# A graph layer's scatter regions: fifteen old pairs in one region of 11 tiles a bucket, read in three parts

## The chip, the cores and the metric

One core of a Trainium2 chip runs the whole kernel. The metric is the time of one execution in device microseconds (us), and the changed kernel is to be compared with the kernel before on it.

## What is computed

One message-passing layer over 3125 nodes of 64 features and 53125 edges (each node has 17 incoming or own edges, sorted by `dst`), all in f32:

```
h = relu(layernorm(x))
msg = concat(h[dst], edge_attr)                 # 53125 x 128
m = relu(msg @ W1a.T + b1a) @ W1b.T + b1b
agg = segment_sum(m, src) / max(count(src), 1)  # by source node
z = relu(concat(h, agg) @ W2a.T + b2a) @ W2b.T + b2b
out = x + concat(z, h) @ Wr.T + br
```

The gather by `dst` is easy, since edges are sorted by it. The sum by `src` is a sum over rows in any order.

## The kernel before

**Groups and pairs.** Edges are worked in 54 groups of 1024, two to a pair, 27 pairs. `ORDER` has a letter for each pair: O for old, C for paired rows. Pairs 0 to 3 are O, then C and O alternate eight times, then seven are O. So groups 8, 9, 12, 13, ..., 36, 37 are C groups, the others O groups.

**The path of a group.** SP loads `dst` (into `dstb`) and the edges (into `eo`). TensorE projects the node window of a pair (`project_windows`), ScalarE copies it to `pw` and makes the window's one-hots in the other half of `eo`; `hidden(g)` is 8 matmuls on TensorE, and `relu(g)` on ScalarE writes their rows to `pay` (old) or `hid` (paired). TensorE and VectorE rank the rows by bucket, of which there are 25 with 125 source nodes each (node modulo 25), and VectorE makes each row's place, `pos_i`. GpSimd then scatters the group's 1024 rows to `slots_dram` in 8 indirect DMAs. In a C group, four `perm` rounds on TensorE bring two rows that go to the same bucket side by side, ScalarE copies them (`copy_unit`), VectorE makes `pos_c` behind the fourth, and GpSimd sends them to `pairs_dram` in 4 indirect DMAs.

**Regions.** `slots_dram` has a region for each of six phases, `PAIRS = [5, 5, 5, 2, 1, 1]` old pairs long; in a region each bucket has `C[ph]` tiles of 128 rows: 4, 4, 4, 2, 1, 1. The paired rows have one region of 3 tiles of double rows a bucket. Since the number of rows that a bucket gets varies, the last `ROOM[ph]` rows of each bucket are cleared first (`clear`, four pieces; `clear_chunks` for the paired), and `check_ranks` sees that each bucket is filled at least to `LEAST[ph]` and not past its end. If a check fails, a slow path computes the layer again; it does not run here.

**Sums.** When a phase's scatters have landed, its region is read back in rounds: `load_round` on SP brings the tiles of 2 or 3 buckets (12 tiles at most, `TPR`) to one of `RR = 4` buffers in `rows`, VectorE makes a one-hot of 128 x 125 for each tile (`hots`), TensorE multiplies one matmul for each tile (`sum_round`), and VectorE adds the round's result to `sums` (`take`). One-hots and results have two buffers, so that round r needs round r - 2 to be done (`hots`) and taken (`sum_round`). Other rounds are `h` and `z` (parts of the output that need no sums), `ccount` and `crank` (ranks of the paired rows), `perm` and `check`.

**What sets the order.** Every engine's program is written out in one order. A planner deals the rounds to groups: `after[g]` are those that come behind `hidden(g)` on TensorE. It has a room in matmuls, fed by 23 a group, by 10 in the first and by -8 behind a C group, and a phase's sums are ready from `END_GROUP[ph] + AFTER_PHASE[ph]`. What doesn't fit is `left_over` and comes behind the last group, and the last phase's rounds are the tail, with the output behind each. On SP, the loads of a group, the clears and the row loads of `after[g - 1]` stand in one queue.

A f32 matmul stands in the trace as two passes (1100 rows at L1252 for 550 sum matmuls). The planner gives the groups around the C groups these sum matmuls before: 24 after 16, 24 after 20, 24 after 24, 12 after 28, 16 after 31, 24 after 36; then 12 after 39, 24 after 40 and 41, 16 after 42, 24 after each of 43 to 48, 6 after 49, 24 after 50 to 52, 28 after 53; 75 are left over in 18 rounds, and 25 are the tail.

## Time and profile before

| | |
|---|---|
| three timed runs, median | 738.26 us (728.47 to 745.05) |
| the profiled execution, its time | 737.99 us |
| its span | 736.3 us |
| mean granted TensorE clock | 0.796 of full |
| PE / PE weight load / DVE / ACT / POOL busy | 66% / 58% / 44% / 38% / 49% |

The span is the part that the hardware profiler records. PE is TensorE, DVE is VectorE, ACT is ScalarE, POOL is GpSimd, SP is the queue that starts most transfers. A row of the timeline gives start, time, engine, line, what is written and read, how many, and in brackets how long the engine stood idle before it and what ended that; "remote" is an end that the trace can't assign, "issue" one without a wait that it shows. Ends of matmuls are modelled, so a row can stand earlier than the result is ready. `oh` is the one-hot tile `oh2`, and `pay<-bank` at L1058 is `copy_unit`.

### The profile page before, as it was taken

The page shows a single profiled execution, that of the slowest core. Times are in us where ns is not written, and L with a number is a line of the kernel's source. Part 1 is how long each engine was busy: PE and PEld are TensorE (multiplying, and loading weights), DVE is VectorE, ACT ScalarE, POOL GpSimd, SP SyncE. Part 2 cuts the span into 40 slices and gives each one's busy share as a digit, 9 for nine tenths or more (in the row PEclk, how much of TensorE's full clock was granted, in tenths as well). Part 3 has the DMA queues.
Part 4 walks back from the last instruction along what each step waited for, and adds up shares of the span by engine and source line. Part 5 has one row for each costly group of instructions (what it writes and reads, how often), then busy time and mean ns, then how long its engine had stood idle before and what let it go on. Part 6 is the DMA issues. An engine that isn't in the chain of part 4 may idle for free.

```text
span 736.3 us, 9578 instructions
## 1 busy us (share of the span) xinstructions
PE 489.4 (66%) x3133; PEld 428.2 (58%) x3133; DVE 325.6 (44%) x1306; ACT 281.1 (38%) x524; POOL 364.3 (49%) x406
## 2 busy tenths in 40 slices
PE   5455369738658478385665865738768876784886
PEld 4344359718456376374554755727758774674775
DVE  7576024214415245043251341614545652573885
ACT  3127326526337245263550761703242343210034
POOL 4766662632725725537355272574656657455000
PEclk9576566859869789598786986968878998797998
DMA  8876655405416227155451651954977866554641
GB/s 196 304 206 180 168 187 161 122 32 186 135 44 223 89 67 260 67 189 169 141 152 51 210 168 59 310 188 142 259 256 236 268 195 229 169 198 137 177 130 47
DMA packets 62323, 123.48 MB, mean 168 GB/s; under 512 B 9369, under 2 KB 33374, under 8 KB 62270
## 3 DMA queue, kind: packets, MB, share of 16 engines
q1 hardware_dynamic: 49598, 91.25, 42.5%
q0 software_dynamic: 12672, 31.58, 12.6%
q8 instruction: 27, 0.44, 0.3%
q14 instruction: 26, 0.21, 0.1%
HBM read 71.53 MB, written 51.25 MB: 167 GB/s over the span
## 4 chain that ended last, share of the span: by engine, by line
PE 52%; issue 23%; DVE 11%; another core or an unknown queue 7%; ACT 5%; DMA 1%; SPq 0%; ACTq 0%; DVEq 0%
PE bank L1252 20%; PE bank L1232 11%; PE bank L1261 9%; DVE oh L771 3%; PE bank L1204 3%; PE bank L1182 3%; ACT pay L1058 1%; PE bank L1285 1%; PE bank L1282 1%; DVE pos L648 1%; DVE slot_t L646 1%; ACT eo L1046 1%; ACT pw L1019 1%; DMA rows<-slots_dram 1%
## 5 line engine op out<-in xcount | busy, mean ns | idle before, releaser
L565 POOL DMA_INDIRECT slots_dram<-pay,pos_i x300 | 293.4, 978 | 148.6 <-issue 89.9
L1252 PE MATMUL bank<-rows,oh 128*125 128x130 f32 x1100 | 179.8, 314 | 110.6 <-issue 92.0
L1252 PEld LDWEIGHTS bank<-rows,oh 128*125 128x125 f32 x1100 | 160.0, 220 | 128.6 <-issue 125.8
L1232 PE MATMUL bank<-pw,eo 128*128 128x128 f32 x856 | 130.2, 310 | 24.8 <-issue 24.1
L548 POOL DMA_INDIRECT pairs_dram<-pay,pos_c x64 | 65.3, 1020 | 161.2 <-DVE pos_c L748 146.5
L1232 PEld LDWEIGHTS bank<-pw,eo 128*128 128x128 f32 x856 | 122.2, 224 | 35.3 <-issue 35.2
L797 DVE TENSOR_TENSOR sums<-sums,bank 125x390 f32<-125x390 f32 (+2 forms) x58 | 29.2, 503 | 204.5 <-remote 148.0
L771 DVE TENSOR_SCALAR oh<-marks,rows 128x125 f32<-128x125 f32 x550 | 114.1, 291 | 3.0 <-DMA rows<-pairs_dram 1.9
L1046 ACT ACTIVATE eo<-dstb,minus_lane 64x256 f32<-64x256 int32 x190 | 85.1, 494 | 54.8 <-issue 27.0
L1261 PE MATMUL bank<-hid,xch 116*128 116x131 f32 (+1 forms) x512 | 69.1, 291 | 21.5 <-ACT pay L1058 13.0
L1035 ACT ACTIVATE pay<-bank 128x1024 f32<-128x1024 f32 (+1 forms) x37 | 37.3, 1007 | 113.2 <-remote 102.4
L1261 PEld LDWEIGHTS bank<-hid,xch 116*128 116x128 f32 (+1 forms) x512 | 65.0, 203 | 25.3 <-ACT pay L1058 15.6
L1051 ACT ACTIVATE eo<-eo,one 64x512 f32<-64x512 f32 x95 | 68.3, 719 | 3.1
L1035 ACT ACTIVATE hid<-bank 128x1024 f32<-128x1024 f32 x16 | 16.4, 1024 | 107.2 <-PE bank L1232 54.3
L1019 ACT COPY pw<-bank 64x512 f32<-64x512 f32 x54 | 31.1, 576 | 66.5 <-remote 63.7
L1182 PE MATMUL bank<-we_in,hT 65*128 65x128 f32 x216 | 37.2, 306 | 18.5 <-issue 18.3
L1182 PEld LDWEIGHTS bank<-we_in,hT 65*128 65x128 f32 x216 | 32.1, 215 | 21.6 <-issue 21.6
L721 DVE TENSOR_SCALAR xch<-slot_no,slot_x 116x256 f32<-116x256 f32 x128 | 37.7, 361 | 0.0
L1058 ACT COPY pay<-bank 128x262 f32<-128x262 f32 x64 | 22.9, 379 | 38.7 <-PE bank L1261 37.3
L748 DVE TENSOR_TENSOR pos_c<-pay,spare 128x4 int32<-128x4 f32 x16 | 2.6, 164 | 75.6 <-ACT pay L1058 75.6
L1282 PE MATMUL bank<-wl,hT 65*125 65x64 f32 x50 | 12.9, 403 | 22.9 <-DVE xr L800 16.2
L1112 ACT ACTIVATE sbar<-tot,cnt 125x128 f32<-125x128 f32 x25 | 8.3, 392 | 47.1 <-DVE cnt L913 47.0
(196 smaller groups left out, 354.7 us busy)
## 6 DMA issues: line engine op xcount, KB each, us to landing
rows<-slots_dram SPq DMA_DIRECT2D x24, 864.0 KB
dstb<-in_dst SPq DMA_DIRECT2D x54, 256.0 KB
eo<-in_edges_T SPq DMA_DIRECT2D x54, 256.0 KB
rows<-pairs_dram SPq DMA_DIRECT2D x12, 864.0 KB
slots_dram<-zeros SPq DMA_DIRECT2D x9, 756.0 KB
slots_dram<-pay,pos_i POOLq DMA_INDIRECT x300
rows<-slots_dram SPq DMA_DIRECT2D x8, 432.0 KB
rows<-slots_dram SPq DMA_DIRECT2D x16, 216.0 KB
```

The costliest lines, as they stand in the source:

```text
L548: pool.indirect_dma_start(out=pairs_dram[:, :], out_offset=bass.IndirectOffsetOnAxis(ap=pos_c[:, u, k:k + 1], axis=0), in_=pay2[:, u, k, : ...
L565: pool.indirect_dma_start(out=slots_dram[:, :], out_offset=bass.IndirectOffsetOnAxis(ap=pos_i[:, u, k:k + 1], axis=0), in_=pay[:, u, k, :] ...
L721: last = V.tensor_scalar(perm[:, n % PR, 256 * t:256 * t + 256], slot_no[0:TILE_A].rearrange("p h s -> p (h s)"), slot_x[0:TILE_A, c // 2 ...
L771: last = V.tensor_scalar(oh2[:, r % 2, t, :], marks[:], rows[:, sum_no[r] % RR, t, MARK:ONE], None, ALU.is_equal)
L1019: A.copy(pw[p, g % WB, :, :], bank[p, 7, :].rearrange("p (k h) -> p k h", h=HID)).then_inc(S["pc"], 1)
L1035: A.activation(target, bank[:, b:b + 2, :].rearrange("p b (k h) -> p (b k) h", h=HID)[:, 0:KT[g], :], ACT.Relu).then_inc(S["rl"], 1)
L1046: last = A.activation(eo[p, g % EB, a * HB:(a + 1) * HB], dstb[p, g % DB // 2, a * HB:(a + 1) * HB], ACT.Square, bias=minus_lane[p, g // 2 ...
L1051: A.activation(e, e, ACT.Relu, scale=-1.0, bias=one[p, :]).then_inc(S["oha"], 1)
L1182: last = T.matmul(bank[:, 7, c * HID:(c + 1) * HID], hT_all[:, n0:n0 + 2 * WS], we_in[0:D + 1, :], start=True, stop=True, skip_group_check ...
L1232: last = T.matmul(bank[:, 2 * (g % 2) + k // 4, (k % 4) * HID:(k % 4 + 1) * HID], eo[:, u, k * 128:(k + 1) * 128], pw[:, g % WB, a, :], st ...
L1252: last = T.matmul(o[0:BN, v * SW:(v + 1) * SW], oh2[:, r % 2, n, :], rows[:, sum_no[r] % RR, n, 0:SW], start=(t == 0), stop=(t == TB[ph] - ...
L1261: last = T.matmul(o[:, side * HW:(side + 1) * HW], perm[0:n, perm_no[r] % PR, 256 * t + 128 * side:256 * t + 128 * side + 128], hid[0:n, c ...
```

## The change

The first three phases become one of 15 pairs with 11 tiles a bucket (`PAIRS = [15, 2, 1, 1]`, `C = [11, 2, 1, 1]`), 275 tiles where there were 300. A table `READS` says in which parts the regions are read: of the new one tiles 0 to 2 once 6 pairs are scattered, tiles 3 to 5 once 11 are, tiles 6 to 10 once 15 are; of the paired region tile 0 once 5 C pairs are, tiles 1 and 2 once all 8 are. `check_early` (three times) sees that every bucket is filled so far. `region` reads tile ranges: 3 tiles of 3 buckets, 5 tiles of 2, 1 or 2 double tiles of 3 in a round. The new region is cleared from groups 12, 14, 16 and 18 on, 352 rows a bucket; the first 10 old pairs may be scattered before that is awaited. The four clears of region 0 among SP's first loads, and the clears of regions 1 and 2, are gone.

```diff
-    PAIRS = [5, 5, 5, 2, 1, 1]
+    PAIRS = [15, 2, 1, 1]
...
-    TB = C + [2 * CT]
+    READS = [(0, 0, 3, 6), (0, 3, 3, 11), (0, 6, C[0] - 6, PAIRS[0])] + [(ph, 0, C[ph], PAIRS[ph]) for ph in range(1, NPH)]
+    READS = READS[:-1] + [(CH, 0, 1, 5), (CH, 1, CT - 1, len(C_PAIRS))] + READS[-1:]
+    NREADS = len(READS)
+    EARLY = [n for n, (ph, t0, nt, pairs) in enumerate(READS) if pairs < (len(C_PAIRS) if ph == CH else PAIRS[ph])]
...
+    TB = [2 * nt if ph == CH else nt for ph, t0, nt, pairs in READS]
...
-    PAIRS_BEFORE_CLEAR = 2
+    PAIRS_BEFORE_CLEAR = 10
     CLEAR_FROM = 6
+    FIRST_CLEARED = [12, 14, 16, 18]
...
-    AFTER_PHASE = [4, 4, 4, 2, 1, 0, 4]
+    AFTER_READ = [4, 4, 4, 2, 1, 4, 4, 0]
...
+            return per[:, t0 * 128:(t0 + nt) * 128, :].rearrange("v (p t) w -> p v (t w)", t=nt)
...
-            sp.wait_ge(S["zero"], 1)
-            clear(0, 0)
             sp.dma_start(wl[:], w_late).then_inc(s_w[1], 16)
             load_dst(4)
-            clear(0, 1)
             sp.dma_start(cols_in[:].rearrange("p a e -> p (a e)"), dst_blocks).then_inc(s_chk, 16)
             load_edges(4)
-            clear(0, 2)
             load_dst(5)
-            clear(0, 3)
             load_edges(5)
...
+                if g in FIRST_CLEARED:
+                    clear(0, FIRST_CLEARED.index(g))
...
+                for n in EARLY:
+                    ph, _, _, pairs = READS[n]
+                    if ph != CH and j == STARTS[ph] + pairs - 1:
+                        check_early(n, row_carry[0:1, 0:NB], base[:, ph, 0:NB], 1.0)
...
+            def check_early(n, row, first, unit):
+                at = EARLY_BAD + EARLY.index(n)
+                link(V.tensor_tensor(region_fill[:, 0:NB], row, first, ALU.subtract))
+                link(V.tensor_reduce(bad[:, at:at + 1], region_fill[:, 0:NB], axis=AX.X, op=ALU.min))
+                link(V.tensor_scalar(bad[:, at:at + 1], bad[:, at:at + 1], unit * (upto_tile(n) - 0.5), None, ALU.is_lt))
```

The planner's rules are the same, fed with the new reads. It now gives, in sum matmuls: none after 16 (four `z` rounds, which stood after 19, 23 and 27, are there), 27 after 20, 9 after 23, 18 after 24, 9 after 27, 12 after 28, 24 after 31, 18 after 32, 8 after 35, none after 36; then none after 39, 27 after 40 and 41, 21 after 42, 24 after 43 to 45, 12 after 46, 16 after 47, none after 48 and 49, 30 after 50, 20 after 51 and 52, 30 after 53; 100 are left over in 21 rounds, and the tail is as before. All in all 525 sum matmuls in 76 rounds for 550 in 67.

TensorE, from the last matmul of the `crank` round after group 31 to the `perm` rounds after group 33 (`hidden` is the row with `pw,eo`, the projection that with `we_in,hT`, sums those with `rows,oh`). Before:

```order
L1204 MATMUL bank<-steps,rows_b 128x425 x2
L1252 MATMUL bank<-rows,oh 125x130 x16
L1232 MATMUL bank<-pw,eo 128x128 x8
L1182 MATMUL bank<-we_in,hT 128x128 x4
L1232 MATMUL bank<-pw,eo 128x128 x8
L1261 MATMUL bank<-hid,xch 128x131 x16
```

The same stretch after the change:

```order
L1241 MATMUL bank<-steps,rows_b 128x425 x2
L1289 MATMUL bank<-rows,oh 125x130 x24
L1269 MATMUL bank<-pw,eo 128x128 x8
L1219 MATMUL bank<-we_in,hT 128x128 x4
L1289 MATMUL bank<-rows,oh 125x130 x18
L1269 MATMUL bank<-pw,eo 128x128 x8
L1298 MATMUL bank<-hid,xch 128x131 x16
```

Eight sum matmuls more stand before `hidden(32)`, and 18 are new between it and `hidden(33)`.

VectorE at the first sums of each kernel, from the end of the `crank` step to the step that makes the last one-hots of the `perm` rounds (`oh` rows are one-hots of sums, `sums` rows the adds, `xch` rows one-hots of `perm`). Before, after group 16:

```order
L669 TENSOR_TENSOR c_parts<-c_carry,c_parts 1x25
L771 TENSOR_SCALAR oh<-marks,rows 128x125 x12
L803 TENSOR_SCALAR zh<-bank,z_bias 128x500
L771 TENSOR_SCALAR oh<-marks,rows 128x125 x12
L797 TENSOR_TENSOR sums<-sums,bank 125x390
L716 COPY hid<-mark 128x8
L717 TENSOR_SCALAR hid<-dest_x 128x8
L721 TENSOR_SCALAR xch<-slot_no,slot_x 116x256 x2
L797 TENSOR_TENSOR sums<-sums,bank 125x390
L721 TENSOR_SCALAR xch<-slot_no,slot_x 116x256 x6
```

And after the change, after group 20:

```order
L696 TENSOR_TENSOR c_parts<-c_carry,c_parts 1x25
L802 TENSOR_SCALAR oh<-marks,rows 128x125 x18
L828 TENSOR_TENSOR sums<-sums,bank 125x390
L802 TENSOR_SCALAR oh<-marks,rows 128x125 x9
L828 TENSOR_TENSOR sums<-sums,bank 125x390
L743 COPY hid<-mark 128x8
L744 TENSOR_SCALAR hid<-dest_x 128x8
L748 TENSOR_SCALAR xch<-slot_no,slot_x 116x256 x2
L828 TENSOR_TENSOR sums<-sums,bank 125x390
L748 TENSOR_SCALAR xch<-slot_no,slot_x 116x256 x6
```

The one-hots of a third round now stand behind the add of the first.

## Rows read from the trace of the kernel before

**Rows 1.** Groups of the page, GpSimd: busy us, mean ns | idle before, releaser

```profile
L565 POOL DMA_INDIRECT slots_dram<-pay,pos_i x300 | 293.4, 978 | 148.6 <-issue 89.9
L548 POOL DMA_INDIRECT pairs_dram<-pay,pos_c x64 | 65.3, 1020 | 161.2 <-DVE pos_c L748 146.5
```

**Rows 2.** Waits, engine GpSimd: us in total, times, longest

```profile
POOL pairs_dram L548 <- DVE pos_c L748: 146.5, 16, 16.6
POOL slots_dram L565 <- issue: 89.9, 284, 1.8
POOL slots_dram L565 <- ACT pay L1035: 51.2, 15, 5.0
POOL pairs_dram L548 <- issue: 14.6, 48, 0.3
```

**Rows 3.** Timeline of GpSimd: first and last scatter, and six first paired scatters

```profile
13.97 1.13 POOL L565 DMA_INDIRECT slots_dram<-pay,pos_i  x1 [7.54 <-ACT pay L1063]
...
222.94 0.96 POOL L548 DMA_INDIRECT pairs_dram<-pay,pos_c  x1 [14.91 <-DVE pos_c L748]
...
271.57 0.96 POOL L548 DMA_INDIRECT pairs_dram<-pay,pos_c  x1 [13.68 <-DVE pos_c L748]
...
319.65 0.96 POOL L548 DMA_INDIRECT pairs_dram<-pay,pos_c  x1 [13.16 <-DVE pos_c L748]
...
365.14 0.96 POOL L548 DMA_INDIRECT pairs_dram<-pay,pos_c  x1 [10.72 <-DVE pos_c L748]
...
413.31 0.96 POOL L548 DMA_INDIRECT pairs_dram<-pay,pos_c  x1 [13.10 <-DVE pos_c L748]
...
461.65 0.96 POOL L548 DMA_INDIRECT pairs_dram<-pay,pos_c  x1 [13.47 <-DVE pos_c L748]
...
673.96 0.96 POOL L565 DMA_INDIRECT slots_dram<-pay,pos_i  x1 [0.30 <-issue]
```

**Rows 4.** Timeline, TensorE and VectorE at the end of a run of scatters

```profile
211.25 3.81 PE L1252 MATMUL bank<-rows,oh 128*125 128x130 f32 x16 [1.04 <-issue]
...
211.45 0.56 DVE L797 TENSOR_TENSOR sums<-sums,bank 125x390 f32<-125x390 f32 x1 [17.32 <-remote]
...
214.86 3.00 PE L1232 MATMUL bank<-pw,eo 128*128 128x128 f32 x16
```

**Rows 5.** Timeline, VectorE and TensorE after groups 31 and 32

```profile
381.48 3.23 DVE L771 TENSOR_SCALAR oh<-marks,rows 128x125 f32<-128x125 f32 x16
...
384.05 5.58 PE L1252 MATMUL bank<-rows,oh 128*125 128x130 f32 x32 [5.33 <-issue]
...
403.35 3.14 PE L1232 MATMUL bank<-pw,eo 128*128 128x128 f32 x13 [0.33 <-issue]
```

**Rows 6.** Timeline, old groups: ScalarE's wait, then first scatters of groups 43, 48 and 50

```profile
534.39 0.90 ACT L1046 ACTIVATE eo<-dstb,minus_lane 64x256 f32<-64x256 int32 x2 [7.25 <-DMA dstb<-in_dst]
...
539.38 0.96 POOL L565 DMA_INDIRECT slots_dram<-pay,pos_i  x1 [1.47 <-issue]
...
606.79 0.96 POOL L565 DMA_INDIRECT slots_dram<-pay,pos_i  x1 [3.33 <-ACT pay L1035]
...
631.71 0.98 POOL L565 DMA_INDIRECT slots_dram<-pay,pos_i  x1 [4.72 <-ACT pay L1035]
```

**Rows 7.** Groups from 674.9 us to the end

```profile
L1252 PE MATMUL bank<-rows,oh 128*125 128x130 f32 x200 | 28.7, 291 | 14.9 <-DVE oh L771 14.7
...
L771 DVE TENSOR_SCALAR oh<-marks,rows 128x125 f32<-128x125 f32 x100 | 21.8, 279 | 0.7 <-DMA rows<-slots_dram 0.6
L797 DVE TENSOR_TENSOR sums<-sums,bank 125x390 f32<-125x390 f32 (+1 forms) x20 | 10.3, 516 | 12.1 <-remote 8.7 <-PE bank L1252 3.1
```

**Rows 8.** Stretch 0 to 50 us (us, PE, PEld, DVE, ACT, POOL, clock, DMA share, GB/s)

```profile
0.00:50.00 50.00, 23.82 (x115) 19.36 (x115) 32.25 (x100) 14.71 (x25) 30.62 (x67) 0.76 0.85 238
```

**Rows 9.** Timeline, a scatter among SP's first clears

```profile
28.24 1.77 POOL L565 DMA_INDIRECT slots_dram<-pay,pos_i  x1 [0.31 <-issue]
```

More of the change, by code:

```diff
@@ L67, in gnn_layer, with expected @@
     FIRST_GROUP = [2 * O_PAIRS[STARTS[ph]] for ph in range(NPH)] + [NG]
-    END_GROUP = [2 * O_PAIRS[STARTS[ph + 1] - 1] + 2 for ph in range(NPH)] + [2 * C_PAIRS[-1] + 2]
-    def expected(ph):
-        edges = sum(min(E_REAL, EDGE0[i + 1]) - EDGE0[i] for i in O_PAIRS[STARTS[ph]:STARTS[ph + 1]])
+    def expected(ph, pairs=None):
+        upto = STARTS[ph + 1] if pairs is None else STARTS[ph] + pairs
+        edges = sum(min(E_REAL, EDGE0[i + 1]) - EDGE0[i] for i in O_PAIRS[STARTS[ph]:upto])
         return edges / NB
@@ L76, in gnn_layer @@
     LEAST = [C[ph] * 128 - ROOM[ph] for ph in range(NPH)]
-    assert all(0 < ROOM[ph] <= min(256, C[ph] * 128) for ph in range(NPH))
+    assert all(0 < ROOM[ph] <= min(512 if ph == 0 else 256, C[ph] * 128) for ph in range(NPH))
     BEGIN = [sum(C[:ph]) * NB * 128 for ph in range(NPH)]
@@ L127, in gnn_layer @@
     ROUNDS_FROM, FULL_FROM, EARLY_SHARE, SHARE, C_SHARE, MOST = 7, 10, 10, 23, -8, 32
-    FIRST_BAD = 4 + 2 * NPH
+    EARLY_BAD = 4 + 2 * NPH
+    FIRST_BAD = EARLY_BAD + len(EARLY)
     rounds = []
     after = [[] for _ in range(NG)]
-    queues = [[v for v in sum_rounds if v[1] != NPH - 1], node_rounds]
+    queues = [[v for v in sum_rounds if v[1] != NREADS - 1], node_rounds]
     def ready(v, g):
         kind, ph = v[:2]
-        return kind != "sum" or g >= END_GROUP[ph] + AFTER_PHASE[ph]
+        return kind != "sum" or g >= END_GROUP[ph] + AFTER_READ[ph]
     room = 0
@@ L165, in gnn_layer @@
     round_of = {n: r for r, n in sum_no.items()}
-    first_round = [min(r for r, v in enumerate(rounds) if v[0] == "sum" and v[1] == ph) for ph in range(NPH + 1)]
+    first_round = [min(r for r, v in enumerate(rounds) if v[0] == "sum" and v[1] == n) for n in range(NREADS)]
     last_perm = [rounds.index(("perm", c, UNITS - 1, 0)) for c in range(len(C_GROUPS))]
@@ L741, in take_chunk_ranks @@
                 link(V.scalar_tensor_tensor(dest_x[:, n % 2, :], slot_x[:, n % 2, :], SCALE / 2.0, wx[:, 1, :], ALU.mult, ALU.add))
+                for m in EARLY:
+                    ph, _, _, pairs = READS[m]
+                    if ph == CH and n == pairs - 1:
+                        check_early(m, c_carry[0:1, :], c_first[0:1, :], float(SCALE))
                 split_row(c_parts, c_carry, 2 * SCALE * SCALE, S["cw"])
```

48 lines of the change are left out of this document (31 added, 17 removed).

## The prediction

> **What bounds the kernel now.** Read the page's two GpSimd groups first, then who GpSimd waited for, then its timeline. GpSimd issues 364 scatters, 300 of old rows and 64 of paired rows, at 0.98 and 1.02 us each [rows 1]; between two of a run lies 0.3 us of issue, 89.9 and 14.6 us in all [rows 2]. So the scatters are 293.4 + 65.3 + 89.9 + 14.6 = 463.2 us. GpSimd's waits add 146.5 us for `pos_c` (16 times), 51.2 us for `relu` (15 times) [rows 2] and 7.5 us at the start [rows 3]. That is 668.4 us, and the last scatter ends at 674.9 us [rows 3] of a span of 736.3: GpSimd's own row of work and waits explains the kernel up to there, within 7 us of set-up, though it is busy for only half the span. The other 61.4 us are the end: left-over rounds and tail. The change leaves all 364 scatters as they are. What it can move is the waits and the end.
>
> How sums enter a wait: look at TensorE and VectorE at 211 us [rows 4]. While GpSimd runs 20 scatters in a row, what TensorE finishes reaches its waiters late: VectorE's `sums` add stood 17.3 us for a round whose matmuls were nearly all issued before the run ended, and was freed at 211.4, 3.4 us after GpSimd's last scatter of that run (the wait that ends at 222.94 began at 208.0). Then the rest of the second round (16 passes, 3.81 us), the next `hidden` (3.00 us) and the `perm` rounds follow, and only behind them `pos_c`, for which GpSimd waits. Six such waits stand in [rows 3]: 14.9, 13.7 and 13.2 us with 24 sum matmuls there (after groups 16, 20, 24), 10.7 with 12 (28), 13.1 with 16 in the group before (31), 13.5 with 24 (36). The last wait is always of this kind, never a load: that is what the stage pays for sums.
>
> **The price of a matmul there.** Mean of the four waits with 24 is 13.8, the one with 12 is 10.7: 0.26 us for each matmul. Without the first of the four, which is over a microsecond above its like, it is 0.23. I take 0.24.
>
> **Part by part.** The profiled execution took 737.99 us, 1.7 more than its span and 0.3 under the median of three; the sum is made on it.
>
> 1. Early clears leave. Four clears of region 0 go out of SP's first 40 us, where the DMA engines are 85% busy [rows 8]; four of region 1 go out of groups 6 to 12. Five MB come back in groups 12 to 18. No wait of GpSimd in that stage ends on a load; the trace shows it by two scatters of 1.77 us in place of 0.96 (one in [rows 9]). Gain 1.6 us; bounds 0 and 5, the larger if `hidden` too is held by traffic.
>
> 2. Waits between the runs of scatters, by what the planner now puts there (the after-order is shown above for groups 30 to 33):
> - after 16: 24 matmuls give way to four `z` rounds, 8 wide passes. The third must wait until the first is taken. I take -1 (bounds -4, as with few matmuls, and +1).
> - after 20: 27 in three rounds for 24 in two. A third round is new: VectorE makes its one-hots only after it has taken the first round, and that is freed at the end of the run [rows 4]. 0.56 + 9 x 0.21 = 2.4 us, then 18 passes at 0.24 = 4.3, so 6.7 in place of 3.8: +2.9.
> - after 23 and 24: 27 for 24, a `z` gone: +0.7. After 27 and 28: 21 for 12: +2.1.
> - after 31 and 32: 42 for 16, in seven rounds for two. By the slope 26 x 0.24 = +6.2. From the other side: in [rows 5] the sums after 31 could start only at 384.05, behind the one-hots, and at the end of the run 13 passes of `hidden` were left. Now at least one more round, a `hidden` and a projection, then three rounds of 12 passes are left on top, some 75 passes at 0.18 (that row's 3.14 / 13 is 0.24, a fast one is 0.13): +13.5. I take +6.2, the measured slope, and keep 13.5 for the range.
> - after 35 and 36: 8 for 24: -16 x 0.24 = -3.8, up to -6 if `perm` rounds fit in the run. I take -4.5.
> Sum: -1 + 2.9 + 0.7 + 2.1 + 6.2 - 4.5 = +6.4.
>
> 3. Old groups 39 to 53. The loop there has 275 sum matmuls for 334. GpSimd waits 3.3 us for `relu` at a typical group [rows 6], 1.5 us where 16 matmuls stood ahead, and nothing where a `relu` came in time (groups 48 and 49 ran as one, then 4.7 us). Groups 46 to 49 now have 12, 16, 0 and 0 for 24, 24, 24 and 6: two waits of 3.3 fall to 1.5, -3.7. Groups 41, 42, 43 and 51 stand behind three rounds (9, 9, 9 twice; 9, 9, 3; 10, 10, 10) where there were two: about +1 each, from the same 1.5 to 3.3. Net 0, bounds -5 and +6.
>
> 4. The end. 100 matmuls in 21 rounds are left over for 75 in 18: the last 25 tiles of the old region, which can't be read before the fifteenth pair. Over the end VectorE's one-hots cost 21.8 us for 100 tiles and its adds 10.3 for 20 [rows 7], and it has no idle time to speak of but the first 8.7 us. 25 x 0.218 + three adds (0.43, 0.43, 0.29) = +6.6; bounds 0, if that idle time takes them, and 8.
>
> 5. Small: two region checks and two base-row matmuls less, three early checks more, all under 1 us of VectorE and beside waits: 0. Nine more loads of rows: 0, since the end's one-hots waited for rows for 0.6 us in all [rows 7].
>
> The Trainium skill speaks against the last point ("DMA: Bandwidth & Descriptors", sections on one DMA's anatomy and on bandwidth): batch transfers to 1 MiB, since each pays about 2 us whatever its size. These loads shrink from 864 KB. By the page, an estimate, nine more of them cost 18 us if nothing hides them; by the row, nothing.
>
> Sum: -1.6 + 6.4 + 0 + 6.6 = +11.4, on 737.99: 749.4. Of the terms only the last has a narrow price, and the matmul slope is drawn from waits that differ in other things too; I say 749.
>
> **Rivals.**
> - Slower: SP's queue becomes the bound. The ring holds four loads; with three rounds a group, SP stands at `round_summed` for a round of the group before instead of the one before that, and the loads of `dst` and edges for later groups queue behind it. For it: ScalarE already waited 7.3 us for `dstb` at 534 us [rows 6], in the group behind a load that waited so. Against it: GpSimd's wait behind that was only 1.5 us. It decides where ScalarE's wait outgrows the 3 us by which `relu` may be late; in the four groups of term 3 the price is at most 7.3 - 3.3 = 4 each. With 3 for each of the four groups: 749.4 + 12 = 761.4. The skill's rule above would come out by this mechanism. Chance 0.27.
> - Faster: all sums taken out of the loop count. 50 matmuls leave it; at 0.24 that is -12, with the start's full -5 and +6.6 at the end: 727.6. For it: the slope is linear over what was seen. Against: the groups relieved most, 48 and 49, already ran without a wait. Chance 0.14.
> - The moved rounds hide in the end's first idle time, where VectorE stood 8.7 us: term 4 is 0, 742.8. Against: that time ends with the results' late arrival, not with work. Chance 0.14.
> - The change doesn't bring reads forward: the first sum round goes from after 16 to after 20. This is in the sum, not a case of its own.
>
> **Chances and range.** Mine has 0.45, own range 742 to 757. The range 727 to 765 takes in most of each rival and the 13.5 of term 2 (756.7), and leaves out the far half of the faster case and what the bounds give only when they fall together. About 2% (14.8 us) is what a measurement of this kernel, whose three runs lie between 728 and 745, tells from no change: under 723 only if the faster case is passed, 0.07; over 753 the slower case and, with the 13.5 of term 2, a part of mine, 0.31; within, 0.62.
>
> **What would show it.** In the profile after: GpSimd's wait before the paired scatters of group 33 near 19 us (13.1 before), of group 37 near 9 (13.5), of group 21 near 16.5 (13.7); first 120 us shorter by 1 to 2; time from the last scatter's end to the end of the span near 68 (61.4). I am wrong in the slope if the wait of group 33 stays at 13 or passes 25; wrong in term 3 if all waits for `relu` sum to other than 46 to 57 us (51.2 before); and the slower case holds if ScalarE waits for `dstb` in the groups behind 40 to 42 and GpSimd's waits there exceed 6 us.

## The result, and the profile after

The changed kernel takes 768.33 us, median of four runs (762.71 to 771.13), where the kernel before took 736.98 (728.47 to 745.05): ratio 1.046, 95% interval 1.039 to 1.053. It is slower by more than twice the 11 us forecast and lies above the range of 727 to 765. Its profiled execution took 762.71 us, with a span of 761.0, 24.7 more than before. The account below is of those 24.7; the other 6 or 7 us of the medians lie between executions. Ratios here and below are made without the few slow executions, so they differ by up to 0.7% from the quotient of the medians.

GpSimd's groups on the page after, to be read beside [rows 1]:

```profile
L588 POOL DMA_INDIRECT slots_dram<-pay,pos_i x300 | 291.2, 971 | 170.0 <-issue 89.9
...
L571 POOL DMA_INDIRECT pairs_dram<-pay,pos_c x64 | 65.0, 1015 | 162.8 <-DVE pos_c L779 148.2
```

And whom GpSimd waited for (us in total, times, longest), beside [rows 2]:

```profile
POOL pairs_dram L571 <- DVE pos_c L779: 148.2, 16, 20.8
POOL slots_dram L588 <- issue: 89.9, 288, 1.7
POOL slots_dram L588 <- ACT pay L1072: 67.3, 10, 15.0
...
POOL slots_dram L588 <- DVE pos_i L678: 5.2, 1, 5.2
```

The scatters cost the same, 2.5 us less. The waits for `pos_c` grew by 1.7 us only, from 146.5 to 148.2. Those for `relu` (with the one for `pos_i`) grew from 51.2 to 72.5: there are fewer of them, 10 for 15, but one is of 11 us and two are of 14 to 15, where the longest before was 5.0. The last scatter ends at 695.4 us (674.9 before), and the end takes 65.6 us for 61.4: 20.4 + 4.3 = 24.7.

GpSimd's timeline shows where, beside [rows 3] and [rows 6]. A wait is named here by the group whose scatters follow it; the prediction's groups 21, 33 and 37 are the waits before the paired scatters of groups 20, 32 and 36, which come behind `hidden` of the next group:

```profile
217.15 0.96 POOL L571 DMA_INDIRECT pairs_dram<-pay,pos_c  x1 [8.48 <-DVE pos_c L779]
...
268.41 0.96 POOL L571 DMA_INDIRECT pairs_dram<-pay,pos_c  x1 [17.21 <-DVE pos_c L779]
...
316.60 0.96 POOL L571 DMA_INDIRECT pairs_dram<-pay,pos_c  x1 [14.39 <-DVE pos_c L779]
...
364.12 0.96 POOL L571 DMA_INDIRECT pairs_dram<-pay,pos_c  x1 [12.84 <-DVE pos_c L779]
...
420.29 0.95 POOL L571 DMA_INDIRECT pairs_dram<-pay,pos_c  x1 [20.85 <-DVE pos_c L779]
...
468.76 0.96 POOL L571 DMA_INDIRECT pairs_dram<-pay,pos_c  x1 [14.76 <-DVE pos_c L779]
...
528.29 0.95 POOL L588 DMA_INDIRECT slots_dram<-pay,pos_i  x1 [14.99 <-ACT pay L1072]
...
665.42 0.96 POOL L588 DMA_INDIRECT slots_dram<-pay,pos_i  x1 [14.31 <-ACT pay L1072]
...
694.39 0.96 POOL L588 DMA_INDIRECT slots_dram<-pay,pos_i  x1 [0.30 <-issue]
```

Six waits before paired groups 16, 20, ... 36, and then the two long ones of the old groups, 41 and 51. From the first scatter of group 36 to that of group 52 the kernel before took 658.4 - 461.6 = 196.8 us, the changed one 678.8 - 468.8 = 210.0. So 13.2 of the 20.4 us are lost in the old groups. In the kernel before, the waits before groups 40 and 41 were short, with 12 matmuls behind group 39 and 24, in two rounds, behind 40:

```profile
501.40 0.96 POOL L565 DMA_INDIRECT slots_dram<-pay,pos_i  x1 [5.00 <-ACT pay L1035]
...
514.71 0.96 POOL L565 DMA_INDIRECT slots_dram<-pay,pos_i  x1 [3.09 <-ACT pay L1035]
```

What stands in the wait before group 41 (all engines; GpSimd's run of 28 scatters ended at 513.3):

```profile
514.01 4.03 SPq L476 DMA_DIRECT2D rows<-slots_dram  x2
514.01 0.56 DVE L828 TENSOR_TENSOR sums<-sums,bank 125x390 f32<-125x390 f32 x1 [28.15 <-remote]
514.49 1.83 DVE L802 TENSOR_SCALAR oh<-marks,rows 128x125 f32<-128x125 f32 x9
...
516.47 4.24 PE L1289 MATMUL bank<-rows,oh 128*125 128x130 f32 x18 [20.37 <-DVE oh L802]
...
518.09 0.50 SPq L421 DMA_DIRECT2D dstb<-in_dst  x1
...
520.50 2.38 PE L1269 MATMUL bank<-pw,eo 128*128 128x128 f32 x16
...
523.30 0.90 ACT L1083 ACTIVATE eo<-dstb,minus_lane 64x256 f32<-64x256 int32 x2 [29.77 <-DMA dstb<-in_dst]
...
526.51 1.02 ACT L1072 ACTIVATE pay<-bank 128x1024 f32<-128x1024 f32 x1
```

Three rounds stand behind group 40. VectorE gets the first round's result only when the run of scatters is over, adds it, makes the third round's one-hots (1.83 us), TensorE multiplies them (4.24), and `hidden(41)` comes after that. TensorE had stood idle for 20.4 us. Beside it, SP's loads of `dst` were sent at 518.1, ScalarE's one-hots came behind them at 523.3, and `relu(41)` behind those at 526.5. Both chains end within a few us of each other: which one was the cause can't be read here.

The end, from 695.4 us on, beside [rows 7]:

```profile
L1289 PE MATMUL bank<-rows,oh 128*125 128x130 f32 x230 | 33.0, 293 | 12.6 <-DVE oh L802 12.4
...
L802 DVE TENSOR_SCALAR oh<-marks,rows 128x125 f32<-128x125 f32 x115 | 24.9, 279 | 2.1 <-DMA rows<-slots_dram 2.0
L828 DVE TENSOR_TENSOR sums<-sums,bank 125x390 f32<-125x390 f32 (+2 forms) x22 | 11.0, 501 | 12.1 <-remote 6.6 <-PE bank L1289 5.1
```

### The profile page after: what moved, and what is told of

It is laid out like the page before. It is cut to its first block, busy times and chain, and to the rows that moved or that the text cites. A ratio compares the mean times of both kernels' runs of the same rounds, so it can differ in the third digit from the quotient of the medians.

```text
span 761.0 us, 9489 instructions
## 1 busy us (share of the span) xinstructions
PE 482.5 (63%) x3081; PEld 425.2 (56%) x3081; DVE 324.6 (43%) x1293; ACT 281.1 (37%) x524; POOL 361.7 (48%) x404
## 4 chain that ended last, share of the span: by engine, by line
PE 34%; another core or an unknown queue 25%; issue 16%; DVE 15%; ACT 8%; DMA 1%; SPq 0%; DVEq 0%; ACTq 0%
PE bank L1289 11%; PE bank L1269 8%; PE bank L1298 7%; DVE oh L802 6%; ACT eo L1083 2%; PE bank L1241 2%; PE bank L1219 2%; ACT pw L1056 1%; ACT eo L1088 1%; ACT pay L1095 1%; DVE pos L671 1%; DVE slot_t L669 1%; DVE sums L828 1%; DMA rows<-slots_dram 1%
## 5 line engine op out<-in xcount | busy, mean ns | idle before, releaser
L1289 PE MATMUL bank<-rows,oh 128*125 128x130 f32 x1050 | 171.9, 321 | 132.1 <-DVE oh L802 77.3
L1289 PEld LDWEIGHTS bank<-rows,oh 128*125 128x125 f32 x1050 | 156.4, 228 | 146.5 <-issue 144.3
L1269 PE MATMUL bank<-pw,eo 128*128 128x128 f32 x856 | 132.0, 310 | 32.1 <-issue 31.6
L571 POOL DMA_INDIRECT pairs_dram<-pay,pos_c x64 | 65.0, 1015 | 162.8 <-DVE pos_c L779 148.2
L828 DVE TENSOR_TENSOR sums<-sums,bank 125x390 f32<-125x390 f32 (+2 forms) x67 | 33.8, 505 | 207.0 <-remote 154.9
L802 DVE TENSOR_SCALAR oh<-marks,rows 128x125 f32<-128x125 f32 x525 | 108.7, 286 | 5.3 <-DMA rows<-slots_dram 2.0
L1298 PE MATMUL bank<-hid,xch 116*128 116x131 f32 (+1 forms) x512 | 71.8, 296 | 22.9 <-ACT pay L1095 12.4
L1298 PEld LDWEIGHTS bank<-hid,xch 116*128 116x128 f32 (+1 forms) x512 | 66.4, 206 | 28.3 <-ACT pay L1095 15.2
L1219 PE MATMUL bank<-we_in,hT 65*128 65x128 f32 x216 | 34.0, 304 | 4.2 <-issue 4.0
```

The source lines that it names most:

```text
L571: pool.indirect_dma_start(out=pairs_dram[:, :], out_offset=bass.IndirectOffsetOnAxis(ap=pos_c[:, u, k:k + 1], axis=0), in_=pay2[:, u, k, : ...
L802: last = V.tensor_scalar(oh2[:, r % 2, t, :], marks[:], rows[:, sum_no[r] % RR, t, MARK:ONE], None, ALU.is_equal)
L828: V.tensor_tensor(sums[:, b0:b0 + m, :], sums[:, b0:b0 + m, :], summed(r), ALU.add).then_inc(S["tk"], 1)
L1219: last = T.matmul(bank[:, 7, c * HID:(c + 1) * HID], hT_all[:, n0:n0 + 2 * WS], we_in[0:D + 1, :], start=True, stop=True, skip_group_check ...
L1269: last = T.matmul(bank[:, 2 * (g % 2) + k // 4, (k % 4) * HID:(k % 4 + 1) * HID], eo[:, u, k * 128:(k + 1) * 128], pw[:, g % WB, a, :], st ...
L1289: last = T.matmul(o[0:BN, v * SW:(v + 1) * SW], oh2[:, r % 2, n, :], rows[:, sum_no[r] % RR, n, 0:SW], start=(t == 0), stop=(t == TB[ph] - ...
```

## The experiments

**Two kinds of executions.** The kernels below ran in sets, each set with the kernel before in it, and each kernel is compared with that one. The kernel before took 737 us in the case's own runs and 743 and 747 in two of the sets, but 529 to 532 in the others. The first are called late here, the others prompt. GpSimd's scatters are the same in both; what differs is how long TensorE's results take to their waiters while GpSimd scatters. VectorE's adds, on the page of the changed kernel in a late execution, and then of the same kernel in a prompt one (after_again):

```profile
L828 DVE TENSOR_TENSOR sums<-sums,bank 125x390 f32<-125x390 f32 (+2 forms) x67 | 33.8, 505 | 207.0 <-remote 154.9
```

```profile
L828 DVE TENSOR_TENSOR sums<-sums,bank 125x390 f32<-125x390 f32 (+2 forms) x67 | 33.7, 503 | 41.7 <-PE bank L1289 41.3
```

The table has, for each kernel, the median of its own runs and of the kernel before in its set, the ratio with its interval, the end of the last scatter, and the time from there to the end of the span, both of the profiled execution.

| kernel | before | this | ratio | last scatter | end |
|---|---|---|---|---|---|
| late: kernel before | | 737.0 | | 674.9 | 61.4 |
| late: changed kernel | 737.0 | 768.3 | 1.046 (1.039 to 1.053) | 695.4 | 65.6 |
| late_two_rounds | 747.5 | 751.4 | 1.012 (1.002 to 1.021) | 679.3 | 68.5 |
| late_rounds_of_8 | 747.5 | 774.0 | 1.043 (1.032 to 1.053) | 707.3 | 61.4 |
| late_loads_ahead | 747.5 | 770.9 | 1.038 (1.028 to 1.048) | 695.9 | 70.0 |
| after_half_buffers (late) | 742.7 | 770.6 | 1.031 (1.021 to 1.040) | 704.1 | 66.8 |
| prompt: before_again | 532.0 | 529.9 | one run | 484.0 | 44.2 |
| after_again | 532.0 | 553.5 | 1.039 (1.030 to 1.047) | 501.9 | 50.0 |
| after_two_rounds | 531.0 | 551.2 | 1.037 (1.030 to 1.043) | 501.7 | 50.2 |
| before_rounds_of_8 | 531.0 | 540.0 | 1.017 (1.010 to 1.024) | 492.6 | 45.4 |
| after_loads_first | 531.0 | 557.6 | no interval | | |
| after_z_split | 531.0 | 555.0 | 1.044 (1.039 to 1.050) | 503.5 | 50.3 |
| after_loads_ahead | 532.0 | 561.3 | 1.055 (1.047 to 1.063) | 505.8 | 54.5 |
| after_paired_once | 532.0 | 542.9 | 1.019 (1.012 to 1.027) | 490.4 | 53.0 |
| after_tile6_early | 531.0 | 553.0 | 1.039 (1.035 to 1.043) | 505.2 | 47.2 |
| after_both_mended | 531.0 | 544.2 | 1.024 (1.019 to 1.029) | 496.1 | 45.2 |
| before_tile_early | 531.0 | 536.0 | 1.005 (1.002 to 1.008) | | |
| late_z_split (prompt) | 529.4 | 552.6 | 1.042 (1.036 to 1.048) | 503.4 | 48.7 |
| before_z_first (prompt) | 529.4 | 544.0 | 1.026 (1.022 to 1.030) | 498.7 | 46.5 |

### The number of rounds behind a group

after_two_rounds and late_two_rounds are one kernel: at most two sum rounds behind a group.

```diff
-            while queue and ready(queue[0], g) and room >= matmuls(queue[0]):
+            while queue and ready(queue[0], g) and room >= matmuls(queue[0]) and (
+                    queue[0][0] != "sum" or sum(rounds[r][0] == "sum" for r in after[g]) < 2):
```

> The changed kernel with one rule more in the planner: at most two sum rounds behind one group. It puts 9+9 after group 20 where three rounds stood, 9+9 after 40, 41, 42 and 43, 10+10 after 50 to 53; 23 rounds with 120 matmuls are left over for 21 with 100. Theory R (a third round costs a way from TensorE to VectorE and back, and the first leg ends only when GpSimd's run of scatters ends): the waits before groups 21, 41, 43 and 51 shrink by 3 to 7 us each, together 12 to 20; the end grows by 20 x 0.22 + 1 = 5.4 us; time 8 to 15 us under the changed kernel's, 753 to 760. Theory C (the sum rounds' place around the paired groups and the early clears are what costs, not the number of rounds): the waits in groups 40 to 53 stay, the end grows, time 768 to 774.

> The kernel of after_two_rounds (at most two sum rounds behind a group), once more, for the case that TensorE's results are late (before near 740). Theory R or S (three rounds in a group make a third one-hot set, and a row load, wait for a result that comes only when the run of scatters ends): the waits of 14 to 15 us before groups 41, 43 and 51 fall to 3 to 5, the stretch from group 36 to group 52 takes 197 to 200 us as in the kernel before (196.8) and not 210; the end is 5 us longer; in all 755 to 762 where the changed kernel takes 768. Theory N (waits follow the number of matmuls): the stretch stays at 207 to 212, the time at 770 or more.

before_rounds_of_8 and late_rounds_of_8 do the reverse to the kernel before: the same 550 matmuls in more rounds. The planner also deals some of them elsewhere for it: 20 behind group 28 for 12, 32 behind 36 for 24, none behind 31 and 39 for 16 and 12.

```diff
-        m = min(512 // SW, TPR // TB[ph])
+        m = min(512 // SW, (8 if TB[ph] == 4 else TPR) // TB[ph])
```

> The kernel before with rounds of 2 buckets, 8 matmuls, in place of 3 buckets, 12, in its regions of four tiles; regions, clears and the 550 matmuls stay. Three or four rounds now stand after groups 16, 24, 36, 40, 41, 42, 50, 52 and 53. Theory R: 3 to 7 us more in the wait behind each of those nine, 15 to 30 us slower in all: 752 to 767. Theory C: only the additional adds and loads of smaller rounds, under 4 us: 737 to 741.

> The kernel of before_rounds_of_8 (the kernel before with three rounds of 8 where two of 12 stood), for the same case. Theory R or S: waits of 10 to 15 us appear behind some of groups 40, 41, 50, 52 and in the paired part, 15 to 30 us slower than before: 755 to 770 for 740. Theory N: 740 to 746.

In late executions the two agree. With two rounds at most, the changed kernel is at 1.012 in place of 1.046, though 120 matmuls are left over for 100 and its end is 2.9 us longer; in its own set, a kernel that keeps the third rounds (late_loads_ahead, below) takes 770.9 us for its 751.4. Group 36 to group 52 takes 660.3 - 464.4 = 195.9 us, as in the kernel before, and the last scatter ends 16 us sooner. With three rounds of 8, the kernel before itself goes to 1.043; its stretch takes 690.8 - 477.8 = 213.0 us, its last scatter ends 32.4 us later, and its end is as before, 61.4. The waits of GpSimd before groups 41 and 51, first of late_two_rounds, then of late_rounds_of_8:

```profile
517.41 1.01 POOL L589 DMA_INDIRECT slots_dram<-pay,pos_i  x1 [8.54 <-ACT pay L1073]
...
650.12 0.96 POOL L589 DMA_INDIRECT slots_dram<-pay,pos_i  x1 [3.40 <-ACT pay L1073]
```

```profile
537.43 1.01 POOL L565 DMA_INDIRECT slots_dram<-pay,pos_i  x1 [14.86 <-ACT pay L1035]
...
677.42 0.96 POOL L565 DMA_INDIRECT slots_dram<-pay,pos_i  x1 [10.20 <-ACT pay L1035]
```

Both kernels have no sums behind group 39, 18 and 24 matmuls behind group 40, and a run of 28 scatters ahead of group 41: the wait is 8.5 us with two rounds (3 to 5 were expected), 14.9 with three. That it isn't the matmuls is shown by the kernel before: 36 of them behind groups 39 and 40, in three rounds with two at most behind one group, and 5.0 + 3.1 = 8.1 us of waits. Behind groups 16 and 24, where late_rounds_of_8 has the same 24 matmuls in three rounds for two, it pays less: 16.1 for 14.9 and 15.2 for 13.2 us. TensorE and VectorE at that place with two rounds (the run ended at 508.9):

```profile
502.80 0.37 PE L1270 MATMUL bank<-pw,eo 128*128 128x128 f32 x1 [1.73 <-issue]
...
511.91 3.69 PE L1270 MATMUL bank<-pw,eo 128*128 128x128 f32 x11 [0.33 <-issue]
...
513.38 0.56 DVE L829 TENSOR_TENSOR sums<-sums,bank 125x390 f32<-125x390 f32 x1 [31.93 <-remote]
```

VectorE's add is as late as ever, 32 us of waiting, but nothing of the group hangs on it. TensorE has gone through both rounds and is inside `hidden` when the run ends. That is the difference: a third round is the only one that needs an answer from VectorE, and that answer came only when GpSimd's run was over: VectorE's add at this place waited 28.2 us in the changed kernel, 31.9 here and 28.5 in late_loads_ahead, and came 0.7, 4.5 and 4.6 us behind the end of the run. In prompt executions the same two edits do less: after_two_rounds is at 1.037 beside after_again's 1.039, and before_rounds_of_8 at 1.017, its loss in waits of 1 to 3 us before paired groups (9, 21, 24, 25, 37). There the old groups go through without a wait of over 1 us, with two rounds and with three. (The expectations for both edits were written for late executions.)

### SP's queue

late_loads_ahead and after_loads_ahead send `dst` and edges of one group further ahead of the row loads; after_loads_first does so only against third rounds.

```diff
+            load_dst(6)
+            load_edges(6)
             for g in range(3, NG):
-                if g >= 6:
-                    load_dst(g)
-                    load_edges(g)
+                if 6 <= g < NG - 1:
+                    load_dst(g + 1)
+                    load_edges(g + 1)
```

> The changed kernel, where SP sends dst and edges of group g + 1, not of group g, ahead of the row loads of after[g - 1]; nothing else is moved. Theory S (SP stands at a row load until a buffer of the ring is free, the loads of dst and edges behind it come late, ScalarE's one-hots wait for them, and relu stands behind those): ScalarE's wait for dstb of 17 us before 286 us falls under 5, GpSimd's waits at groups 32 and 33 fall from 13 us in all under 5, and the time falls by 7 to 12 us against after_again. Theory R (the number of rounds costs by itself): the waits and the time stay within 2 us.

> The kernel of after_loads_ahead (dst and edges of group g + 1 stand ahead of the row loads of after[g - 1]), for the same case. Theory S: ScalarE's waits of 29, 30 and 10 us for dstb, which end 7 to 10 us after the run of scatters has ended, are gone; the waits before groups 33, 41 and 51 fall by 4 to 9 us each; 750 to 762 where the changed kernel takes 768. Theory R (the third round by itself): each falls by at most 2 us, 764 or more.

> The changed kernel, where SP sends the loads of dst and edges of the next group before the row load of a third or later round, which waits for a buffer. Theory S (SP's queue: ScalarE's one-hots stand behind loads that are sent late, and relu behind them): ScalarE's waits for dstb of 29 us before 407 and 523 us vanish, the waits of GpSimd before groups 33, 41 and 51 fall by 3 to 8 us each, 10 to 20 us faster than the changed kernel, 748 to 758. Theory R: the waits stay within 1 us each, since relu and the one-hots are freed only by TensorE's late results: 765 to 770.

after_half_buffers gives the rounds of 6 tiles half a buffer each, so that eight can be on their way.

```diff
+        small = rounds[r][1] == 5
+        halves = [(at + k) % (2 * RR) for k in range(1 if small else 2)]
...
-                if sum_no[r] >= RR:
-                    sp.wait_ge(S["ag"], round_of[sum_no[r] - RR] + 1)
+                if waits_for[r] is not None:
+                    sp.wait_ge(S["ag"], waits_for[r] + 1)
```

> The changed kernel, where a round of the paired region's early read, 6 tiles, takes half a buffer of 12: up to eight of them are on their way, so that SP never stands at one of the seven row loads for groups 31 and 32. Order and number of everything else stay. Theory S (SP's stand at the fifth of these loads, 17.8 us, makes the loads of dst and edges late, ScalarE's one-hots wait for them and relu stands behind those): ScalarE's wait of 16.8 us for dstb at 284 us is gone, relu of group 32 runs when TensorE has its hidden rows, 6 us earlier, the wait at group 32 falls from 10.1 to 4 or 5 us, time 546 to 549 for after_again's 553. Theory A (the 42 matmuls and their adds are themselves what is late; loads_ahead, which took the wait for dstb away but sent the rows later, gained 4 of 13): at most 2 us of the 13.4 at groups 32 and 33 go, time 551 to 553.

late_loads_ahead took away what it aimed at: ScalarE's waits for `dstb` of 29.1, 29.8 and 9.6 us became 2.8 and two that no longer appear (one of 8.6, at 560 us, is new). GpSimd gained nothing in the old groups. Its wait before group 41, with what VectorE and ScalarE do ahead of it:

```profile
516.47 0.56 DVE L830 TENSOR_TENSOR sums<-sums,bank 125x390 f32<-125x390 f32 x1 [28.53 <-remote]
...
525.53 1.02 ACT L1074 ACTIVATE pay<-bank 128x1024 f32<-128x1024 f32 x1 [28.48 <-PE bank L1271]
...
527.32 0.96 POOL L590 DMA_INDIRECT slots_dram<-pay,pos_i  x1 [15.41 <-ACT pay L1074]
```

ScalarE had its one-hots by 497; `relu` now waits for TensorE, which itself stood 14.8 us for the third round's one-hots, and GpSimd's wait is 15.4 us for 15.0. From group 36 to group 52 it takes 212.1 us for 210.0, and the last scatter ends at 695.9 for 695.4. Only the wait before group 32 fell, from 20.8 to 16.9 us. after_half_buffers, late as well, took the wait for `dstb` at that group away too and gained 2.3 us there (18.6); its groups 41, 43 and 51 waited 15.3, 14.1 and 14.4 us (group 43 waited 5.2 in the changed kernel; the edit leaves the order of work there as it was, and whether the edit or the execution makes that difference is open). So SP's queue is worth 2 to 4 us at group 32, and nothing in the old groups. In a prompt execution the place looks like this, in after_again (SP stands at a row load from 255.6 on):

```profile
273.45 3.84 SPq L476 DMA_DIRECT2D rows<-pairs_dram  x3
...
284.08 0.91 ACT L1083 ACTIVATE eo<-dstb,minus_lane 64x256 f32<-64x256 int32 x2 [16.84 <-DMA dstb<-in_dst]
...
298.69 0.95 POOL L571 DMA_INDIRECT pairs_dram<-pay,pos_c  x1 [10.14 <-DVE pos_c L779]
```

With the loads ahead (after_loads_ahead) the two waits, before groups 32 and 33, are 4.3 and 5.0 us for 10.1 and 3.3, but VectorE waits 52.6 us for rows in place of 14.0, and the kernel as a whole is slower, 1.055. That theory S would give 7 to 12 us was wrong there by sign. after_loads_first shows neither gain nor loss: its four times lie between 547.5 and 559.6 us.

### The early read of the paired region, and the end

after_paired_once undoes the early read of the paired region; after_tile6_early leaves 75 matmuls over for 100; after_both_mended has that and starts the early read at group 36.

```diff
-    READS = READS[:-1] + [(CH, 0, 1, 5), (CH, 1, CT - 1, len(C_PAIRS))] + READS[-1:]
+    READS = READS[:-1] + [(CH, 0, CT, len(C_PAIRS))] + READS[-1:]
```

```diff
-    READS = [(0, 0, 3, 6), (0, 3, 3, 11), (0, 6, C[0] - 6, PAIRS[0])] + ...
+    READS = [(0, 0, 3, 6), (0, 3, 3, 11), (0, 6, 1, 13), (0, 7, C[0] - 7, PAIRS[0])] + ...
-    AFTER_READ = [4, 4, 4, 2, 1, 4, 4, 0]
+    AFTER_READ = [4, 4, 4, 4, 2, 1, 10, 4, 0]     # after_tile6_early: 4 for the 10
```

> The changed kernel with one part undone: the paired region is read once, when all eight pairs are scattered, so the seven rounds after groups 31 and 32 and the two after 35 are gone, and groups 47 to 49 get 12+12, 12+12, 12+6. Theory S and the prediction's term for groups 31 to 36 agree here: the waits at groups 32 and 33 fall to under 4 us in all, and the time by 8 to 12 us against after_again; what is left over before is then the end (+5 us) and the rest. If the early read of the paired region isn't what costs: within 3 us of after_again.

> The changed kernel with the last read of the long region split: tile 6 once 13 pairs are scattered (nine rounds of 3 matmuls after groups 47 and 48, where room was left), tiles 7 to 10 once 15 are. Left over are then 75 matmuls in 18 rounds, as in the kernel before, for 100 in 21. Theory of the end (each matmul left over costs VectorE's one-hot, 0.22 us, each round its add): the time from the last scatter's end to the end of the span falls from 50.0 us (after_again) to 44 to 45; the last scatter ends within 2 us of after_again's 501.9; 546 to 549 us for 553. If the end is ruled by something else, it stays at 50.

> The same, and the early read of the paired region starts six groups later, so that its nine rounds stand after groups 36, 39 and 40, not after 31, 32 and 35. If the losses of the change are the rounds before the paired groups 32 and 33 and the 25 matmuls more at the end, and nothing else, both are gone: waits at groups 32 and 33 under 2 us (13.4 in after_again), a wait of up to 5 us at group 37 in their place, last scatter's end 486 to 491, end 44 to 45, time 531 to 538 for 532 of the kernel before. If the early read costs wherever it stands, the waits move to groups 36 to 41 and the time stays over 541.

> The kernel before once more, for its profile beside the others of this call. The runs of the call before took 531 us for it, where the case's took 737: if that comes back, GpSimd's waits for pos_c, 146.5 us, and for relu, 51.2 us, must be nearly gone (under 25 us in all), the last scatter ends near 485 us and the end takes near 45.

> The changed kernel once more. Where before takes 531: 548 to 556 us, ratio 1.035 to 1.045, by 8 to 15 us more of GpSimd's waits (at groups 32 and 33 above all) and 4 to 6 more at the end. Where before takes 737: 762 to 771.

In prompt executions GpSimd hardly waits at all. Its waits in before_again, and then in after_again:

```profile
POOL slots_dram L565 <- ACT pay L1063: 7.6, 1, 7.6
POOL pairs_dram L548 <- DVE pos_c L748: 3.0, 2, 2.7
POOL slots_dram L565 <- ACT pay L1035: 1.2, 4, 0.3
```

```profile
POOL pairs_dram L571 <- DVE pos_c L779: 20.1, 6, 10.1
...
POOL slots_dram L588 <- ACT pay L1100: 7.6, 1, 7.6
```

The change costs 501.9 - 484.0 = 17.9 us up to the last scatter there, 13.4 of them before groups 32 and 33, where 42 matmuls in seven rounds stand for 16 in two; and 5.8 at the end. Read once, the paired region costs nothing at that place (no wait of GpSimd over a microsecond there), the last scatter ends 11.4 us sooner, and the kernel gains 10.6 us. With both mended it is 9.3 us faster than after_again and still 2.4% behind the kernel before: the end is down to 45.2, but the last scatter still ends 12.1 us late, in waits of 1 to 3 us before groups 17, 24, 25, 29, 36, 37 and 48; all but the last are paired groups, with more rounds or other ones near them than in the kernel before; which of these cost what was not tested. That the two parts were all, as expected, was wrong. after_tile6_early shortened the end by 2.8 us, not by 5 to 6, and lost as much to a later last scatter (505.2 for 501.9), with a wait of 1.7 us before group 47. There SP stood for 18.2 us among the row loads for the rounds of 3 matmuls, and this time its queue is what GpSimd waited for:

```profile
409.83 18.21 SPq L476 DMA_DIRECT2D rows<-slots_dram  x5
428.09 0.50 SPq L421 DMA_DIRECT2D dstb<-in_dst  x1
...
433.88 0.90 ACT L1083 ACTIVATE eo<-dstb,minus_lane 64x256 f32<-64x256 int32 x2 [17.29 <-DMA dstb<-in_dst]
...
438.88 0.96 POOL L588 DMA_INDIRECT slots_dram<-pay,pos_i  x1 [1.66 <-ACT pay L1072]
```

### Ideas of the change put into the kernel before

```diff
     # before_tile_early: third region of 5 pairs, tile 0 read after 3 of them
+    READS = [(0, 0, C[0], 5), (1, 0, C[1], 5), (2, 0, 1, 3), (2, 1, C[2] - 1, 5)] + ...
```

```diff
     # before_z_first
-    AFTER_PHASE = [4, 4, 4, 2, 1, 0, 4]
+    AFTER_PHASE = [8, 4, 4, 2, 1, 0, 4]
```

> The kernel before, with one idea of the change put where the end can gain by it: of its third region tile 0 is read once 3 of its 5 pairs are scattered (25 matmuls in nine rounds after groups 49 and 50), the other three after the fifth; nothing else is changed. Left over are 69 matmuls in 17 rounds for 75 in 18. By the end's price 2 us less there; nine small rounds more in the loop, which costs nothing while GpSimd runs without a wait. 529 to 532 us for 532 of the kernel before: a gain of 0.3% at most, likely not to be told from none.

> The kernel before with AFTER_PHASE[0] = 8 for 4: the four z rounds come behind group 16 and the first region's sums start behind group 20, as in the changed kernel, with rounds of 12, two at most. By the changed kernel's waits: 6 us less at group 16; group 24 gets 12 matmuls behind 23 more, group 28 24 for 12: 3 to 5 us more each. Between 4 us less and 4 us more, 0.995 to 1.005 of the kernel before; where results aren't late, no difference.

Neither helps. before_tile_early is the changed kernel's code with the old regions and clears; it has nine rounds more, tile 0 in small ones and the rest of that region in rounds of 9 for 12. They cost 0.5% in a place that was thought free, against 6 matmuls fewer at the end. The `z` rounds put first cost 2.6%, where no difference was expected: with 12 matmuls behind 23, 24 behind 28 for 12, and 12 and 4 behind 31 and 32 for 16 behind 31, there are waits of 2.8, 2.7, 3.0 and 2.7 us before groups 24, 25, 29 and 33, where before_again has none, and the last scatter ends 14.7 us later. No kernel tried beats the kernel before.

### What the lateness goes by

after_z_split and late_z_split are one kernel: the same columns of the `z` rounds in more passes.

```diff
-                    last = T.matmul(o[:, 0:m * BN].rearrange("p (b i) -> p b i", i=BN), w2a_h, hT_bucket[0:D, b0:b0 + m, :],
-                                    start=True, stop=True, skip_group_check=True)
+                    for v in range(m):
+                        last = T.matmul(o[:, v * BN:(v + 1) * BN], w2a_h, hT_bucket[0:D, b0 + v, :], start=True, stop=True,
+                                        skip_group_check=True)
```

> The changed kernel with each z matmul of up to 500 columns split in up to four of 125: the same columns in 26 passes for 8 to 14, nothing else. Theory P (while scatters run, TensorE gets done about one pass per 0.7 to 1.2 us, whatever its width): the wait before group 17, where four z rounds stand, grows from 8.5 us by 18 passes, 5 to 13 us more (part of it hidden in the run), and the time by 5 to 13. If it is columns or busy time that counts: the wait and the time stay within 1 us.

> The kernel of after_z_split (each z matmul of up to 500 columns as up to four of 125), for the case that TensorE's results are late. If they are late by a time for each pass (0.6 to 0.8 us a pass of 128 columns in the changed kernel's run of scatters before group 16), the 18 passes more of the four z rounds behind group 16 lengthen the wait there from 8.5 us to 14 to 20. If they are late by columns (the wide passes there took 1.4 to 2.5 us each by the same records), the wait stays within 1.5 us.

Both times the executions were prompt, so neither answers the question. They show only that 18 narrow passes more cost about a microsecond when results are prompt (waits of 2.1 and 1.4 us before group 17, 0.9 in after_again).

## Why the prediction was wrong

**What bounds the kernel** was right: GpSimd's row of scatters and waits accounts for 20.4 of the 24.7 us, the end for 4.3.

**Term 1, the start (-1.6).** Nothing came. Group 8's first scatter came at 124.3 us for 122.1, behind a run of 24 scatters and a wait of 10.95 us before group 7. late_rounds_of_8, whose clears stand at the start and whose program is that of the kernel before up to group 16, has that wait too (10.9) and started group 8 at 125.9 us. So it isn't the clears, and 3.8 us lie between two executions of the same start: a gain of 1.6 could not be seen. In prompt executions group 8 started at 98.2 us for 96.9.

**Term 2, the waits between the runs (+6.4).** The sum was right and its parts were not. Over the six pairs of waits, from groups 16, 17 to 36, 37, it came to +7.0: +9.5 in the first waits of the pairs, which follow here, and -2.5 in the second, for which the prediction has no price. So that the sum fits is in part luck. Group 16: -6.4 for -1 (four `z` rounds are much cheaper than 24 sum matmuls, 8.5 us where the bound gave 10.9). Group 20: +3.5 for +2.9; the third round's way back to VectorE was priced here, about rightly. Groups 24 and 28: +1.2 and +2.1 for +0.7 and +2.1. Group 32: +7.7 for +6.2, inside the bound of 13.5; in prompt executions the place cost 13.4. Group 36: +1.3 for -4.5. The mistake there was to count matmuls and not where they stand: the 8 that are left stand behind group 35, ahead of `hidden(36)`, and ScalarE's `relu(36)` waited until 457.2, after the run, for a result that TensorE had issued by 441.6. In the kernel before, `hidden(36)` had nothing ahead of it, and `relu(36)` ran at 430.1, within the run:

```profile
457.20 1.02 ACT L1072 ACTIVATE hid<-bank 128x1024 f32<-128x1024 f32 x1 [21.03 <-PE bank L1269]
```

**Term 3, the old groups (0, bounds -5 and +6).** This is the step that failed, by 13 us. Its words were: "Groups 41, 42, 43 and 51 stand behind three rounds [...] where there were two: about +1 each, from the same 1.5 to 3.3." The price of a third round that term 2 took from [rows 4], a way to VectorE and back that opens only at the end of a run, holds here too, and more of it: where no rounds stand behind a group (39, 48, 49), the next group's `relu` comes in time, GpSimd goes on for 24 or 28 scatters, and the whole of the work then stands in one wait. Added up from the two timelines: groups 40 and 41 waited 15.0 us for 8.1, 42 and 43 9.7 for 5.1, 48 to 51 19.6 for 11.4, in all +19.7 where the four third rounds were put at +4; groups 44 to 47 waited 8.1 for 14.2, so the relief was real, -6.1 where -3.7 stood. (The loop had 326 matmuls there before, not the 334 of the prediction.) late_two_rounds takes the third rounds away and has 195.9 us for the stretch; late_rounds_of_8 adds them and has 213.0.

**Term 4, the end (+6.6).** Right in kind, +4.3 in size (bounds 0 and 8). VectorE's one-hots there grew by 3.1 us, its adds by 0.7, and its first idle time fell from 8.7 to 6.6. The page's counts say why it was less than 6.6: 115 one-hots for 100 stand in the end, not 125, since ten of the 25 more were made before the last scatter had ended, and a part of the rest hid in the idle time. By late_two_rounds too, 45 matmuls more than the kernel before cost 7.2 us, 0.16 each and not 0.26.

**Term 5** was right: the end's one-hots waited 2.0 us for rows, for 0.6 before. The Trainium skill ("DMA: Bandwidth & Descriptors", section on the anatomy of one DMA) gives its 2 us of fixed cost for transfers that GpSimd issues; these loads are SP's. The prediction's 18 us from it, for nine loads that nothing hides, don't show: the waits for rows in the end grew by 1.4 us.

**The signs.** The wait before group 32 was 20.8 us (near 19 forecast), the one before group 20 17.2 (near 16.5), the one before group 36 14.8 (near 9); the end took 65.6 us (near 68). The waits for `relu` came to 67.3 us, or 72.5 with the one for `pos_i`, outside the 46 to 57 that the prediction had set as the bounds of term 3.

**The rivals.** The slower case, 761.4 with a chance of 0.27, was nearest, and its sign appeared behind group 40, though not behind 41 and 42 (waits of 3.5 and 5.2 us): ScalarE waited 29.8 us for `dstb` there, and GpSimd 15.0. But the sign was not the cause. late_loads_ahead removed it and left GpSimd's wait as it was. The third round holds both, TensorE's way to `hidden` and, by the buffer that it doesn't set free, SP's loads; taking the second away only lays the first bare. The other two rivals fell. No case had both the third round's full price and the old groups together; with 13 for term 3 the sum would have been 762, the profiled execution's time to a microsecond, but that would be luck too, with errors in terms 1, 2 and 4 that cancel.

## What to carry to other kernels

When results are late in one stretch, count the round trips that must end in it, not the work: two rounds that need no answer cost their matmuls, a third that needs one costs a wait until the stretch ends, with all that stands behind it. Here that was 7 us where the stretch was 28 scatters long, and 1 to 2 us behind groups 16 and 24. Smaller parts that are ready sooner mean more rounds; if their number behind a step exceeds the buffers, the gain in tiles is lost in handshakes. And a wait that shows beside the critical one can be its consequence: test it by taking it away, with what feeds it left alone.
